# Attention's steady part: the value blocks of a round stand behind score pairs 1, 3 and 6 (256, 256, 512 columns) instead of 2, 5 and 7 (512, 256, 256)

## The reference

```python
xn = _layernorm(x, axis=-1)
x = x + _L0_attn_ref(xn, Wq, bq, Wk, bk, Wv, bv, Wo, bo) + _L0_ffn_ref(xn, Wg, Wu, Wd, Wr, temperature)
```

```python
q = (hidden_states @ Wq.T + bq).reshape(b, s, HEADS, HEAD_DIM)       # k and v likewise
scores = jnp.einsum('bqhd,bkhd->bhqk', q * SCALE, k)
probs = jax.nn.softmax(scores, axis=-1)
out = jnp.einsum('bhqk,bkhd->bqhd', probs, v).reshape(b, s, d)
return out @ Wo.T + bo
```

## Time and profile before

| | us |
|---|---|
| median of three runs | 6256.24 |
| the profiled execution's own time | 6257.91 |
| its span, first to last instruction | 6256.2 |
| PE busy | 6164.1 (99%) |
| DVE (VectorE) busy | 5534.3 (88%) |
| ACT (ScalarE) busy | 4839.5 (77%) |
| mean granted TensorE clock | 0.988 |

### The profile page before, as it was taken

The page is one execution under the profiler, slowest core; times in us unless marked ns, Lnnn a source line. Parts: engine busy times, 40 slices in busy tenths (PEclk is TensorE's granted clock), DMA queues, the critical chain, the costliest instruction groups (busy, mean ns, idle before and its releaser), DMA issues. The chain is left out here.

```text
span 6256.2 us, 120429 instructions
## 1 busy us (share of the span) xinstructions
PE 6164.1 (99%) x48392; PEld 3144.9 (50%) x48392; DVE 5534.3 (88%) x8291; ACT 4839.5 (77%) x9075; POOL 524.3 (8%) x540
## 2 busy tenths in 40 slices
PE   8999999989999999999999999999999999999998
PEld 7888888844444444444444444444444444444444
DVE  5555555479999999999999999999999999999993
ACT  4333333319888898888888888888889888888896
POOL 3222222200000000000000000000000000000000
PEclk9999999969999999999999999999999999999999
DMA  3111111121111111111111111111111111111113
GB/s 100 48 48 49 49 48 48 39 32 29 34 34 34 35 32 30 30 31 30 31 31 30 31 30 31 30 31 30 30 30 31 36 33 33 34 35 36 32 50 129
DMA packets 243448, 244.68 MB, mean 39 GB/s; under 512 B 159616, under 2 KB 204416, under 8 KB 236544
## 3 DMA queue, kind: packets, MB, share of 16 engines
q1 hardware_dynamic: 231864, 206.04, 15.1%
q0 software_dynamic: 11024, 30.94, 2.1%
HBM read 159.26 MB, written 76.58 MB: 38 GB/s over the span
## 5 line engine op out<-in xcount | busy, mean ns | idle before, releaser
L1042 DVE TENSOR_REDUCE mx<-sc 128x1 f32<-128x512 f32 (+1 forms) x6144 | 4783.2, 846 | 13.8 <-PE sc L915 13.5
L1022 ACT ACTIVATE pr<-st 128x512 f32<-128x512 f32 x8120 | 4266.3, 603 | 483.7 <-PE st L928 480.1
L915 PE MATMUL sc<-experts 48*128 48x512 f32 x8192 | 2825.9, 446 | 22.6 <-DVE mx L1042 13.8
L928 PE MATMUL st<-experts 50*128 50x512 f32 x8120 | 2699.1, 432 | 0.1
L936 PE MATMUL pv<-pr,vst 128*32 128x256 f32 (+1 forms) x24440 | 2398.8, 464 | 2.1 <-ACT pr L1022 0.9
L928 PEld LDWEIGHTS st<-experts 50*128 50x128 f32 x8120 | 1308.1, 184 | 1828.9 <-ACT pr L1022 1654.5
L915 PEld LDWEIGHTS sc<-experts 48*128 48x128 f32 x8192 | 1330.1, 186 | 92.6 <-DVE mx L1042 75.0
L936 PEld LDWEIGHTS pv<-pr,vst 128*32 128x32 f32 x24440 | 481.8, 108 | 958.2 <-issue 915.6
L449 ACT ACTIVATE gated<-gate 128x512 f32<-128x512 f32 x256 | 152.2, 599 | 565.9 <-PE up L75 565.5
L671 DVE TENSOR_TENSOR hraw<-gated,up 128x512 f32<-128x512 f32 x256 | 174.5, 686 | 415.3 <-ACT gated L449 403.0
L75 PE MATMUL down<-experts,hid 128*128 128x256 f32 x3072 | 390.1, 283 | 15.0 <-POOL hid L499 15.0
(11 more groups left out here) (111 smaller groups left out, 1298.6 us busy)
## 6 DMA issues: line engine op xcount, KB each, us to landing
experts<-parts_d SPq DMA_DIRECT2D x372, 256.0 KB, 4.3
parts_d<-part SPq DMA_DIRECT2D x64, 512.0 KB, 2.8
x_in<-in_L_attn_hidden_states SPq DMA_DIRECT2D x16, 512.0 KB, 4.7
v_d<-v_sb SPq DMA_DIRECT2D x32, 256.0 KB, 2.1
vst<-v_d SPq DMA_DIRECT2D x128, 64.0 KB, 2.2
sums_d<-oT SPq DMA_DIRECT2D x256, 32.0 KB
whole<-sums_d POOLq DMA_DIRECT2D x32, 256.0 KB, 3.0
recs<-rden_d POOLq DMA_DIRECT2D x32, 256.0 KB, 5.5
```

Of the source, the lines that this page charges most:

```text
L915: nc.tensor.matmul(sc_bank(g % RINGB), qr[par][r0:r0 + TERMS, q0:q0 + P], kr[par][r0:r0 + TERMS, b * GT:(b + 1) * GT], start=True, stop=Tr ...
L928: nc.tensor.matmul(score_bank(at, x), kr[par][r0:r0 + ROWSM, kb * P:(kb + 1) * P], qr[par][r0:r0 + ROWSM, q0:q0 + GT], start=True, stop=Tr ...
L1022: nc.scalar.activation(pr[:, (QSUB * kb + j) % PRING, :], score_bank(2 * at + q, x), ACT.Exp).then_inc(st_read, 1)
L1042: nc.vector.reduce_max(mx[par][:, t, i:i + 1], sc_bank(first, n), AX.X).then_inc(sc_read, 1)
```

## The change

The three calls of `values` in a round are put behind other pairs, and the even key block is now the one that is split in halves:

```diff
@@ -980,12 +980,12 @@
                             score(s, BANKS * r + i, par, hf, here, 0)
                             if not (last and to >= 2 * heads):
                                 max_bank(((s + 1) * QT + t) * BANKS + i, t % QT, i, to // 2 % RING, to % 2, 1)
-                            if i == 2:
-                                values(2 * r, 0, GT)
-                            if i == 5:
-                                values(2 * r + 1, 0, GT // 2)
-                            if i == 7:
-                                values(2 * r + 1, GT // 2, GT)
+                            if i == 1:
+                                values(2 * r, 0, GT // 2)
+                            if i == 3:
+                                values(2 * r, GT // 2, GT)
+                            if i == 6:
+                                values(2 * r + 1, 0, GT)
```

## The result

The changed kernel takes 6294.68 us (median of 4 runs, 6293.06 to 6297.61) against 6256.44 (4 runs, 6254.44 to 6257.73): a ratio of 1.0062, 95% interval 1.0049 to 1.0075. It is slower by 38 us; 6293 was predicted. The profiled execution has a span of 6291.3 us, the one before 6256.2.

A forecast was written before the change was run, and what follows sets the result against it. The prediction took VectorE's gapless reductions as the bound. Steady rounds 0, start 0 and 62 borders x 0.60 = 37 us, added to 6256, gave 6293 us; range 6280 to 6308, to hold 8 in 10.

The forecast's parts named there:

- VectorE sets the pace and has no gaps: Steady rounds: VectorE's reductions run in a row at 4.654 us a round; TensorE alone would need 4.57.
- The turned ring is free: Steady rounds: the same ring of pieces, turned by four pairs, meets the same reductions and exponentials; cost 0.
- The chain of 1.71 or 1.67 from pair 7: Super step border: us from pair 7's start through exponential and copy to the value block.
- TensorE at the block after 0.96: Super step border: TensorE reaches the waiting half block 0.96 us after pair 7's start and stands still 0.73 us.
- Slack 0.13: VectorE's two-bank reduction: the matmul it needs may be 0.13 us late at no cost, 0.20 less 0.07 of wake-up.
- Loss of 0.60 a border, one loss covering the other: Super step border, round 1: VectorE loses 0.73 - 0.13 = 0.60 us, including 0.33 at pair 2's reduction.
- two losses: Rival at the border: losses at pair 2 and at pairs 4 and 5 add, 0.93 us each border, 6314; chance 0.06.
- Start 0, 2 us either way: Program start, TensorE at its lower clock: the new order costs 0, with 2 us either way.
- The clock stays: Border pauses: granted clock stays 1.00; the rival, a lower clock after each pause, gave 6475, chance 0.02.
- What would show it: Expected trace signs: 62 waits of some 0.7 us, VectorE idle some 37 us more, super steps of 75.3 us.
- The bounds 6282 and 6306: Whole time under the forecast: 6288 to 6301 us, widened by 2 to 4 us for start and misread slack.
- the second tie: Border: score 3 of round 1 needs only pair 0's exponential, claimed done before TensorE gets there.

The follow-up runs named there:

- e3: The changed kernel with ScalarE's copy of pv to oT ahead of, not behind, the exponential of pair 7 of round 0: 6255.5 us, ratio 1.0000.
- e7: The new order of value blocks in super step 0 alone, the order of the kernel before everywhere else: 6257.3 us, ratio 1.0001.
- e4: The changed kernel with the two half blocks of round 1 behind pairs 2 and 4, not 1 and 3: 6287.5 us, ratio 1.0047.
- e6: The changed kernel with the two half blocks of round 1 behind pairs 3 and 4, not 1 and 3: 6318.6 us, ratio 1.0098.
- e8: e3 with one extra ScalarE instruction of 128 x 256, result unread, ahead of the copy: 6270.8 us, ratio 1.0023.
- e9: e3 with two extra ScalarE instructions of 128 x 256, results unread, ahead of the copy: 6287.7 us, ratio 1.0052.

## Why the prediction was right

- *VectorE sets the pace and has no gaps:* right. Outside round 1 the changed kernel has VectorE late by no more than 0.003 us a super step.
- *The turned ring is free:* right, by e3 (74.96 us a super step in the new order, 74.98 in the old).
- *The chain of 1.71 or 1.67 from pair 7:* measured 1.72 in super step 20, 1.69 in the median. *TensorE at the block after 0.96:* it is there in e3 at 0.96 and stands still for 0.73 after, as predicted.
- *Slack 0.13:* right, though it was read at a single border; with it the table above gives the loss of kernels that are up to 1.16 late.
- *Loss of 0.60 a border, one loss covering the other:* 0.61; the copies lie 75.34 us apart, where 75.3 was predicted and 74.74 is before. The two gaps in the starts are 0.33 and 0.26, and their sum is the whole but for 0.02 (the reduction behind each wait takes 0.01 longer). I had priced "two losses" as 0.33 + 0.60; the 0.33 is part of the 0.60, and the traces have it so.
- *Start 0, 2 us either way:* the traces of after and e7 have super step 0 shorter by 1.5 us, with an earlier rise of the clock, inside the bounds. The median of e7 shows no gain, and a cause isn't shown. The prediction had looked for such a gain in the places of the blocks and not in the clock.
- *The clock stays:* right. 40 pauses of 0.7 us in 3000 us, and 1.00 granted throughout. The swing of the clock that the Trainium skill tells of where TensorE idles shortly and frequently between groups of matmuls ("TensorE: Matmul & The Clock Gate", "A second HAM failure mode: psum-queue depth-cycling") did not come with pauses this rare; more frequent ones were not tried.
- 62 x 0.61 is 38 us, which is the difference of the medians; the spans differ by 35, since the profiled execution was 3 us ahead when super step 1 began.
- *What would show it:* VectorE's idle time was to grow by 37 us and grew by 25, because the view leaves out the overlap of the rows, as said above; by the starts the forecast holds. The bounds 6282 and 6306 stand 6 and 5 us outside 6288 and 6301, a little more than the 2 to 4 us given for them; nothing hangs on it.

Where I went wrong is in the expectations behind it: four of them (e4, e6, e8, e9) took the wait for the copy as the only tie to ScalarE. The prediction had checked the second tie (score 3 of round 1 on the exponential of pair 0) for its own case, where the waiting half block stands in between and TensorE comes after the exponential. With the block behind that score (e6), with one pair fewer in between (e4, pair 4 on the exponential of pair 1) or with ScalarE later (e8, e9) TensorE runs into it.

## What to carry to other kernels

An issue order can be turned around a ring without cost and still lose where the ring is cut: at the hand-over between two steps, count what lies between the instruction that starts the other engine's chain and the one that waits for its end, and move the other engine's part forward as well (here that took the 38 us away). In this kernel, whose two engines are within 2% of each other, a late instruction cost its lateness at the next matmul that the pacing engine needs, less the slack that one border of the trace showed. Work that fills a wait may also keep a second wait closed, so before it is moved, follow each instruction behind it to what it waits for.

## What the hardware showed that was not expected

- A score pair that starts after a wait, or right behind a value block, takes 0.49 to 0.50 us instead of 0.39. After a wait, the next pair follows 0.33 later instead of 0.23, and a value block 0.43 instead of 0.33. A wait of 0.02 so cost 0.12 (e8).
- The wake-up after a copy's end was 0.05 us where TensorE's block waited for that alone and 0.10 where the list also had the wait for the values in front, in every kernel where the block waited for the copy.
- ScalarE's copy, when it waits for nothing else, starts 0.08 us after the rows of the whole block end (e3); an extra 128 x 256 instruction cost 0.31 from start to start (e8), against 0.48 for 128 x 512.
- TensorE's clock rose earlier in all eight traces whose super step 0 doesn't have the old order in rounds 0 and 1 (20.8 to 23.9 us after the first `nm` reduction, against 27.1 to 30.9 in the other three), though TensorE is busy without a gap up to the rise in before and after alike. Why isn't known.
